# Third attention of a four-layer stack: the transposes and projections of a step in one row behind its scores and values

## The reference, cut to what matters

```python
# L2_xattn, 16 heads of 64; query = layernorm(x), key = value = ctx_1024 (4 x 1601 x 128)
scale = HEAD_DIM ** (-0.5)
q = (query @ w_q).reshape(B, Q, HEADS, HEAD_DIM).transpose(0, 2, 1, 3)
k = (key @ w_k).reshape(B, Kl, HEADS, HEAD_DIM).transpose(0, 2, 1, 3)
v = (value @ w_v).reshape(B, Kl, HEADS, HEAD_DIM).transpose(0, 2, 1, 3)
scores = jnp.einsum('bhqd,bhkd->bhqk', q, k) * scale
attn = jax.nn.softmax(scores, axis=-1)
out = jnp.einsum('bhqk,bhkd->bhqd', attn, v)
out = out.transpose(0, 2, 1, 3).reshape(B, Q, HEADS * HEAD_DIM)
return out @ w_o
```

## Time and profile before

| | us |
| --- | --- |
| median of three executions | 2186.76 |
| lowest and highest | 2182.64, 2189.31 |
| profiled execution, its own time | 2189.7 |
| its span, first to last instruction | 2187.9 |
| PE busy in it | 1919.4 (88%) |
| third attention, first to last score matmul | 832.5 to 1640.6 |
| ACT waiting in the third attention for transposes (L2384 for L2293) | 327.7 |

### The profile page before, as it was taken

How to read it: one execution, slowest core, us unless ns; L and a number is a source line. 1 busy time by engine, 2 the same in 40 slices (tenths; PEclk the granted TensorE clock), 3 DMA queues, 4 the chain that set the end, 5 groups by cost and what they waited for, 6 DMA issues and landing times. The chain is left out here.

```text
span 2187.9 us, 43812 instructions
## 1 busy us (share of the span) xinstructions
PE 1919.4 (88%) x17168; PEld 1359.0 (62%) x17168; DVE 1314.1 (60%) x3233; ACT 1287.5 (59%) x2062; POOL 135.3 (6%) x354
## 2 busy tenths in 40 slices
PE   5999999956739459999999999999994689999997
PEld 3677777734625356777777777777772446666663
DVE  5888888867436325554555455545546667666662
ACT  3899999944329124555555555555553346666664
POOL 4000000000023110000000000000000400000000
PEclk9899999976959579999999999999996779999998
DMA  6111111101071340000000000000000611111110
GB/s 227 54 43 44 46 45 45 37 16 69 8 180 24 106 122 1 1 1 1 1 1 1 1 1 1 1 1 1 1 1 12 187 56 50 46 45 41 46 40 17
DMA packets 54811, 88.89 MB, mean 41 GB/s; under 512 B 9897, under 2 KB 31453, under 8 KB 54609
## 3 DMA queue, kind: packets, MB, share of 16 engines
q1 hardware_dynamic: 52993, 81.32, 12.8%
q0 software_dynamic: 1616, 4.79, 0.6%
HBM read 67.52 MB, written 18.55 MB: 39 GB/s over the span
## 5 line engine op out<-in xcount | busy, mean ns | idle before, releaser
L2384 ACT ACTIVATE a_prT<-bank 128x512 f32<-128x512 f32 (+1 forms) x448 | 232.7, 565 | 327.9 <-PE bank L2293 327.7
L1204 DVE CUSTOM_DVE_ANT_0 a_attn_junk<-wide,a_mask 128x801 f32<-128x801 f32 (+1 forms) x256 | 247.5, 991 | 122.0 <-PE wide L1036 121.8
L1147 ACT ACTIVATE a_attn_prT<-bank 128x512 f32<-128x512 f32 (+1 forms) x448 | 237.1, 566 | 121.8 <-PE bank L1053 109.1
L2409 DVE CUSTOM_DVE_ANT_0 a_sc<-wide,a_zeros 128x1024 f32<-128x1024 f32 (+1 forms) x256 | 243.1, 988 | 91.4 <-PE wide L2279 91.4
L1485 DVE CUSTOM_DVE_ANT_0 a_attn_sc<-wide,a_mask 128x801 f32<-128x801 f32 (+1 forms) x256 | 252.9, 989 | 11.7 <-PE wide L1340 9.9
L1356 PE MATMUL bank<-ident,a_attn_sc 128*128 128x128 f32 x1664 | 245.1, 276 | 14.8 <-ACT a_attn_prT L1444 13.8
L1356 PEld LDWEIGHTS bank<-ident,a_attn_sc 128*128 128x128 f32 x1664 | 199.1, 142 | 61.9 <-issue 42.2
L2293 PE MATMUL bank<-ident,a_sc 128*128 128x128 f32 x1664 | 231.2, 277 | 1.5 <-ACT a_prT L2384 1.5
L2293 PEld LDWEIGHTS bank<-ident,a_sc 128*128 128x128 f32 x1664 | 185.4, 141 | 54.4 <-issue 28.1
L2279 PE MATMUL wide<-a_kT,a_qT 64*128 64x512 f32 (+1 forms) x1024 | 211.0, 529 | 0.0
L1450 ACT ACTIVATE a_attn_sc<-a_attn_sc,a_attn_nmx 128x1601 f32<-128x1601 f32 x128 | 209.4, 1636 | 2.2 <-DVE a_attn_nmx L1491 2.1
(11 more groups left out here) (456 smaller groups left out, 2546.8 us busy)
## 6 DMA issues: line engine op xcount, KB each, us to landing
a_ks<-a_k_parts SPq DMA_DIRECT2D x384, 75.0 KB
a_k_parts<-a_proj_kp SPq DMA_DIRECT2D x24, 416.0 KB, 4.2
a_qx<-a_q_stack SPq DMA_DIRECT2D x384, 12.0 KB
moe_w1b<-in_e_w SPq DMA_DIRECT2D x15, 256.0 KB, 2.9
ctxT<-in_ctxT SPq DMA_DIRECT2D x4, 832.0 KB, 10.6
a_ctxn<-in_ctxn SPq DMA_DIRECT2D x4, 832.0 KB
m_q_stack<-m_proj_qp POOLq DMA_DIRECT2D x9, 256.0 KB, 4.5
m_ks<-m_k_parts SPq DMA_DIRECT2D x24, 96.0 KB
```

What stands on the lines that cost most here:

```text
L1147: act.activation(prT[0:keys, u % PRT, kt:kt + m, :], bank_of(s, f"W{g}")[0:keys, 0:m * S].rearrange("p (t q) -> p t q", q=S), ACT.Exp).the ...
L1204: dve.tensor_tensor_reduce(junk[:, n % 2, 0:w], S_WIDE[n % 2][:, 0:w], mask(qt, at, w), 1.0, LOWEST, ALU.add, ALU.max, mx[:, p % 2, qt, e, ...
L2384: copy = lambda out, src: act.activation(out, src, ACT.Copy)
L2409: dve.tensor_tensor_reduce(sc[:, s % 2, h, at:at + w], S_WIDE[h][:, 0:w], zeros[:, 0:w], 1.0, LOWEST, ALU.add, ALU.max, mx[:, s % 2, h, p: ...
```

## The change

The items that stood between the two score halves now stand behind the second half. TensorE's turn is: first score half, values, second score half, then all items in one row. The table starts with O instead of having it seventh, so that items get other numbers: X0 and X1 move from ring bank 2 to bank 0, T0 and T2 from bank 0 to bank 1, T1 and T3 from bank 1 to bank 2; T4, T5, X2, T6 and X3 keep theirs. Who empties which item stays the same. VectorE takes X1 behind the second score half, no longer ahead of it. No instruction is added or removed.

```diff
-    SLOTS = ("T0", "T1", "X0", "T2", "T3", "X1", "O", "T4", "T5", "X2", "T6", "X3")
-    BY_ACT = {0, 1, 2, 3, 4, 7, 8, 10}
+    SLOTS = ("O", "T0", "T1", "X0", "T2", "T3", "X1", "T4", "T5", "X2", "T6", "X3")
+    BY_ACT = {1, 2, 3, 4, 5, 7, 8, 10}
...
                     values(s)
-                for k in range(0, 6):
-                    emit(s, k)
                 if 0 <= s < STEPS:
                     scores(s, 1)
-                for k in range(6, 12):
+                for k in range(len(SLOTS)):
                     emit(s, k)
...
-                take(dve, dve.tensor_copy, scaled, s, 5, freed_by_dve)
...
-                    dve.wait_ge(item_ready, made[s, 6])
+                    dve.wait_ge(item_ready, made[s, 0])
...
                     dve.tensor_reduce(nmx[:, s % 2, :], mx[:, s % 2, :, :], X, ALU.max, negate=True).then_inc(max_ready, 1)
+                take(dve, dve.tensor_copy, scaled, s, 6, freed_by_dve)
                 take(dve, dve.tensor_copy, scaled, s, 9, freed_by_dve)
                 take(dve, dve.tensor_copy, scaled, s, 11, freed_by_dve)
```

More of the change, by code:

```diff
@@ L2385, in _ @@
             for s in range(-2, STEPS + 2):
-                for k in (0, 1, 2, 3, 4, 7, 8, 10):
+                for k in sorted(BY_ACT):
                     take(act, copy, None, s, k, freed_by_act)
@@ L2430, in _ @@
                     dve.wait_ge(added, 2 * t + 1)
-                    dve.scalar_tensor_tensor(tile, RING[6 % 3][:, 0:P], rtot[:, t % 2, 1:2], tile, ALU.mult,
+                    dve.scalar_tensor_tensor(tile, RING[0][:, 0:P], rtot[:, t % 2, 1:2], tile, ALU.mult,
                                              ALU.add).then_inc(added, 1)
```

## The result

The kernel after took 2198.59 us, the median of five executions between 2194.12 and 2200.12 us; the kernel before, run beside it, 2189.17 us. The ratio is 1.0047 with a 95% interval of 1.0028 to 1.0067: 9.4 us slower, where 8.3 was forecast. The intervals overlap, so the whole times alone place the loss only between 6 and 21 us. The traces place it better, because a large part of the spread lies in other layers: the first matmul of this attention stands at 820.30 us in the profile before and at 813.11 in the one after, though nothing ahead of it was changed.

What follows compares the result with a forecast made beforehand. TensorE, busy without a gap at full clock, was taken as the bound. Steady turns +1.8 us and edges +6.5 made 8.3 us, on 2186.76 a forecast of 2195.1 us; range 2184 to 2202.

Steps and rivals of the forecast that it cites:

- The steady turn: Turns 2 to 61: an odd turn goes from 12.68 to 12.71 us, 0.03 more, 1.8 us over 60 turns.
- The new wait: Steady turns: X2 stands in X1's bank and waits 0.18 us for VectorE's copy of X1.
- the price of a change of shape: TensorE: each change of array shape costs some 0.10 us on leaving and 0.05 to 0.1 on entering.
- the first rival: Steady turns: no new wait, only the lost change of shape counts; -9.0 us, 2184.3 us in all; 11%.
- the second: Steady turns: values to scores costs nothing on leaving, -0.10 us a turn from the forecast, 2189.1 us; 15%.
- X0 and X1: Steady odd turn: X0 takes 1.00 us with a wait of 0.16, X1 0.98 with a wait of 0.09.
- Turn 0: Without values, the second scores wait for the first half's drain: 11.0 us against 7.73, +3.3.
- Turn 1: Transposes but no values to cover the drain: 11.82 us against 9.58, +2.2.
- Turns -2 and -1: Projections alone, three of four now in one bank: +0.6 us, between 0 and 2.
- X3 and the next X0 wait less: Projection-only turns: X2 waits about 1.0 us for X1's copy, these two less, one row showing 0.65.
- Turn 62 to the end: Last turns, transposes without projections alternating between two banks, then O waiting for its operand: together +0.4 us.
- ScalarE as the bound: Rival: ScalarE limits the unbroken row of items; 0.2 us a turn, +12, 2207 us; 14%.

Runs made afterwards that it cites:

- e1: The kernel after with O between T0 and T1 instead of ahead of T0; 2210.05 us, ratio 1.0100 to the kernel before.
- e4: The kernel after with item order O, T0, X0, T1, X1, T2, X2, T3, X3, T4, T5, T6, ScalarE emptying nine; 2176.74 us, ratio 0.9951 to the kernel before.
- e7: The kernel after, unchanged, measured once more; 2200.79 us, ratio 1.0075 to the kernel before.

## Why the prediction was right, point by point

- **The steady turn.** Forecast 12.71, measured 12.71; +0.03 a turn, measured 0.024. The new wait came where it was named, behind VectorE's copy of X1, and the price of a change of shape was confirmed twice, by 2.99 for the values and by e1. As both terms were nearly equal, the net is small, but each alone would have been 9 to 11 us: the first rival (waits don't grow) and the second (values to scores for nothing) were both wrong in the row they named. The rule of the Trainium skill that a change of tiling mode drains the engine (TensorEngine Tiling (Array Packing), Key Properties) agrees with this cost of 0.15 us each, though no row shows a drain as such; taken alone it would have given the wrong sign.
- **X0 and X1.** Waits as before (1.00 and 0.97), as forecast.
- **Turn 0.** +3.4 against 3.3. The named chain (drain, ScalarE's copy, VectorE's copy) stands in the rows. The forecast let the whole second half start 4.45 us into the turn and take 1.23; in fact the first head's part started at 3.30 and the second head's waited inside the row. The half was over at 5.67 against 5.68: the sum was right, its split was not.
- **Turn 1.** The mechanism was right, the size was not: +3.8 against 2.2. The 1.6 more are matmuls at the lower clock behind the idle time. The step that failed is that I costed TensorE's idle time at its own length alone.
- **Turns -2 and -1.** +2.4 against 0.6, above even the 2 that I gave as a bound. The term "X3 and the next X0 wait less" was mis-sized. In both profiles the first matmuls of the stage run at the lower clock: the granted clock has a mean of 0.72 between 820.3 and 832.5 before (first line) and of 0.64 between 813.1 and 827.8 after, which is 6.8 and 10.6 us at the lower level.

```profile
820.30:832.50 12.20, 10.18 (x36) 5.72 (x36) 4.06 (x8) 1.19 (x2) 0.00 (x0) 0.72 0.00 0
813.10:827.80 14.70, 11.69 (x38) 6.67 (x38) 3.96 (x8) 1.19 (x2) 0.00 (x0) 0.64 0.00 0
```

TensorE was idle for 2.0 us before and 3.0 after (the stretch less PE's busy time), and busy for 10.2 and 11.7 with the same projections (the two records more in the second line are of turn 0's scores). So, as an estimate, 1.0 of the 2.4 is longer waits for banks, not far from the 0.6, and 1.5 is matmuls at the lower clock, for which the forecast had no term. In e4, whose table has no common banks there, the clock is 0.79 between 812.9 and 822.0, 3.8 us at the lower level. That the waits delay the clock's rise fits these three lengths (3.8, 6.8, 10.6), but the kernel before has one profile only, and no run tests it.
- **Turn 62 to the end.** +0.4 as forecast.
- **ScalarE as the bound.** Didn't happen: in the kernel after it waits for the transposes inside the row of items, and in e4, with nine items and not eight, the turns got shorter.
- **The whole.** The terms came to 8.3, the stage shows 11.5, and the two comparisons 1.0047 and 1.0075 lie on both sides of it (1.0053). The missing 3.2 is the clock's part in turn 1 (1.6) and the term of the turns ahead (1.8), less 0.4 in the steady turns. That the first comparison gave 9.4, so near the forecast, is in part luck: the terms are 3.2 short of the stage, and e7 gave 15.6.

## What to carry to other kernels

On a full engine an order that saves a change of shape is worth its price only if the items left side by side don't meet in a buffer: for each buffer, sum the work between the end of one use and the next, and compare it with the time until it has been taken out. Work that stands between two dependent pieces is cover; before gathering pieces, look at the first and last passes of the loop, where the other cover is missing, and move the order of every engine that serves them, not TensorE's alone. Two turns of 64 held most of this loss.

## What the runs showed of the hardware that I had not expected

- TensorE's lower clock came behind short idle times and into a full stretch. Two waits for a drain of some 2.5 us (1.32 of each as idle time in the rows), with two of 0.7 to 0.8 between, were followed by 3.4 us at 1.2 GHz in the profiles of the kernel after and of e7 (0.57 and 0.58 as the mean of 4 us). That cost 1.6 us, in addition to the idle time. In e1 the same waits came with 10.3 us at that level. The Trainium skill (TensorE: Matmul & The Clock Gate, A second HAM failure mode: psum-queue depth-cycling) tells of a bf16 kernel whose matmul groups idle briefly between them, while they cycle through PSUM banks, so that the clock swings. The runs agree for these first turns, in fp32; the steady turns, with waits of 0.08 to 0.18 us for the same banks, stay at 1.00.
- Leaving one shape of the array for another cost 0.09 to 0.10 us in each pair that a row without the change stood beside, 64-column to 64-row work among them, where each uses half of the array. For scores to values no such row stands in these kernels.
